# Mask attention phase: lift by a reduction, later store, the bias behind chunk 0's low halves, and a new order of small steps

## The reference

```python
xq = layer_norm(x, qn_w, qn_b)
ctx = layer_norm(context, cn_w, cn_b)
q = (xq @ q_w).reshape(B, N, H, D)            # H = 16 heads of D = 32
k, v = ...                                     # ctx @ kv_w
attn = jnp.einsum('bnhd,bmhd->bhnm', q, k) * scale
attn = softmax(jnp.where(xa_mask[:, None], neg, attn))
out = jnp.einsum('bhnm,bmhd->bnhd', attn, v).reshape(B, N, C)
x = x + (out @ proj_w + proj_b)
```

## Time and profile before

| what | value |
|---|---|
| median of three runs | 2689.25 us |
| the profiled execution | 2689.7 us, its span 2687.7 us, 2.0 us around it |
| mean granted TensorE clock | 0.992 |
| busy, share of the span | TensorE 97%, VectorE 74%, ScalarE 58%, GpSimd 34% |

### The profile page before, as it was taken

How to read it: one execution, slowest core, us unless ns; L and a number is a source line. 1 busy time by engine, 2 the same in 40 slices (tenths; PEclk the granted TensorE clock), 3 DMA queues, 4 the chain that set the end, 5 groups by cost and what they waited for, 6 DMA issues and landing times.

```text
span 2687.7 us, 67270 instructions
## 1 busy us (share of the span) xinstructions
PE 2602.1 (97%) x23144; PEld 2232.5 (83%) x23144; DVE 1983.5 (74%) x5443; ACT 1561.2 (58%) x4742; POOL 923.5 (34%) x1097
## 2 busy tenths in 40 slices
PE   5999999998999999999999999999999999999997
PEld 4777887886888888888888888888788888888886
DVE  6899999996544434443468888887788888888877
ACT  5777777776211111111267777777677676766764
POOL 4666666672100000000103333333433433434331
PEclk8999999999999999999999999999999999999999
DMA  5666676673402111111221111112321222212210
GB/s 163 164 159 162 172 175 160 170 203 88 130 32 63 47 47 37 56 47 47 79 87 48 47 47 52 49 47 79 98 81 62 79 79 76 87 62 89 75 47 24
DMA packets 313622, 236.12 MB, mean 88 GB/s; under 512 B 150736, under 2 KB 240848, under 8 KB 312656
## 3 DMA queue, kind: packets, MB, share of 16 engines
q1 hardware_dynamic: 313552, 235.22, 30.7%
HBM read 137.65 MB, written 63.96 MB: 75 GB/s over the span
## 4 chain that ended last, share of the span: by engine, by line
PE 76%; DVE 9%; ACT 8%; issue 5%; DMA 1%; POOL 1%; SPq 0%; DVEq 0%; ACTq 0%; POOLq 0%
PE cross_work L181 17%; PE mlp_acc L3308 13%; PE mlp_f L3290 13%; PE causal_work L181 10%; ACT mask_prob_even L964 3%; PE cross_scores L2301 3%; PE cross_scores L2278 2%; PE cross_attended L2331 2%; PE causal_scores L2301 2%; PE mask_work L181 2%; DVE mask_scores L1556 2%; PE causal_scores L2278 2%; PE causal_attended L2331 2%; ACT mask_prob L964 2%; PE cross_probsT L2301 1%
## 5 line engine op out<-in xcount | busy, mean ns | idle before, releaser
L3083 ACT ACTIVATE mlp_h<-mlp_f,mlp_b1col 128x512 f32<-128x512 f32 x128 | 88.3, 690 | 525.9 <-PE mlp_f L3290 525.9
L3290 PE MATMUL mlp_f<-mlp_xT_hi,mlp_w 128*128 128x512 f32 x1024 | 335.4, 389 | 0.9 <-DVE mlp_xT_lo L3176 0.9
L3190 DVE CAST mlp_hT_hi<-mlp_h 128x512 fp32r<-128x512 f32 x128 | 58.1, 454 | 369.9 <-ACT mlp_h L3083 369.8
L3308 PE MATMUL mlp_acc<-mlp_w,mlp_hT_hi 128*128 128x512 f32 x1024 | 315.2, 389 | 0.0
L964 ACT ACTIVATE cross_prob<-cross_scores,cross_low 128x256 f32<-128x256 f32 x512 | 237.1, 489 | 63.6 <-DVE cross_low L1550 63.6
L964 ACT ACTIVATE causal_prob<-causal_scores,causal_low 128x128 f32<-128x128 f32 (+1 forms) x512 | 210.3, 437 | 93.6 <-DVE causal_low L1556 93.6
L3290 PEld LDWEIGHTS mlp_f<-mlp_xT_hi,mlp_w 128*128 128x128 f32 x1024 | 192.3, 188 | 42.1 <-DVE mlp_xT_lo L3176 1.3
L3308 PEld LDWEIGHTS mlp_acc<-mlp_w,mlp_hT_hi 128*128 128x128 f32 x1024 | 192.2, 188 | 40.0
L181 PE MATMUL causal_work<-causal_xT_hi,causal_w 128*128 128x256 f32 x1008 | 217.0, 293 | 0.3 <-DVE causal_qk_parts L1506 0.3
L1556 DVE CUSTOM_DVE_ANT_0 mask_scores<-mask_scores,mask_mask 128x256 f32<-128x256 f32 x512 | 200.7, 452 | 21.8 <-PE mask_scores L2278 10.0
L731 POOL TENSOR_SCALAR causal_q<-all_own_head,causal_qk_parts 128x128 fp32r<-128x128 f32 x128 | 60.4, 483 | 406.0 <-DVE causal_qk_parts L1506 395.6
(11 more groups left out here) (368 smaller groups left out, 8108.9 us busy)
## 6 DMA issues: line engine op xcount, KB each, us to landing
cross_x_in<-after_attention SPq DMA_DIRECT2D x17, 512.0 KB, 4.1
mask_x_in<-in_x SPq DMA_DIRECT2D x16, 512.0 KB, 4.3
mask_c_in<-in_ctx SPq DMA_DIRECT2D x16, 512.0 KB, 4.8
mask_res<-in_x SPq DMA_DIRECT2D x16, 512.0 KB, 4.1
after_attention<-mask_res SPq DMA_DIRECT2D x16, 512.0 KB, 3.1
mlp_x<-after_attention SPq DMA_DIRECT2D x8, 1024.0 KB, 5.5
mlp_stage<-in_L_xattn_fc_w SPq DMA_DIRECT2D x8, 1024.0 KB, 5.6
after_layer<-mlp_y SPq DMA_DIRECT2D x8, 1024.0 KB, 4.3
```

The source lines that it names most:

```text
L3290: ins = pe.matmul(F1[m % 2][:], W[2 * (m // 4)][:, a, k, m % 4 * P:(m % 4 + 1) * P], xT[p][:, k, :], start=(k == 0 and n == 0), stop=(k == ...
L3308: ins = pe.matmul(ACC[t][:], hT[a][:, m % 2, t * P:(t + 1) * P], W[2 * (m // 4) + 1][:, p, m % 4, :], start=(m == 0 and n == 0), stop=(m = ...
```

## The change

Nothing that is computed changes. Its parts:

1. `low` gets a second column that GpSimd fills once with 10, and `lift` becomes a reduction over the pair (`tensor_reduce`, add) in place of `tensor_scalar`.
2. SyncE issues `cross_over(b, 2)` before `store(b - 1)`.
3. GpSimd does `add_bias(b)` behind `low_halves(b, 0)`, so in front of `values_left(b)`.
4. VectorE, loop: `normed(b, -1)`, `qk_lo(b, 1)`, `post_lo(b, 0)` instead of `post_lo(b, 0)`, `qk_lo(b, 1)`, `normed(b, -1)`; and `project(b, 0)` in front of `minima(b, 2)` instead of behind it.
5. ScalarE: `post_hi(b, 1)` in front of both `high_halves(b, 0, ...)`; in turn 0 the parts of v (`values`, `values_high`, `values_middle`) are made where the loop makes them, instead of later.
6. TensorE: `turn_sums(b, -1)` in front of `values(b, 1)` instead of in its middle; turn 0 makes `values(0, 1)` whole.
7. Opening: `front(1)` in front of `minima(0, 0)`, and `values(0, 0)` and `qk(0, 1)` earlier among the first exponentials. In turn 0 the first two `turn_over` stand in front of `minima(0, 2)`. In turn 15 the places where the MLP's opening may enter move.

```diff
-        low = r("low", [P, 4, TT])
+        low = r("low", [P, 4, TT, 2])
...
+            if crossing:
+                cross_over(b, 2)
             if not cross and prev:
                 store(b - 1)
-            if crossing:
-                cross_over(b, 2)
...
+            pool.memset(low[:], LIFT).then_inc(s["pool_chain"], 1)
...
                 low_halves(b, 0)
+                if prev:
+                    add_bias(b)
                 values_left(b)
...
+                post_hi(b, 1)
             high_halves(b, 0, 0)
-            if prev:
-                post_hi(b, 1)
             high_halves(b, 0, 1)
...
-            dve.tensor_scalar(lifted[:, h, :], low[:, h, :], LIFT, None, ALU.add).then_inc(s["lifted"], 1)
+            dve.tensor_reduce(lifted[:, h, :], low[:, h], AX_X, ALU.add).then_inc(s["lifted"], 1)
...
+            if prev:
+                minima(b, 0)
+                normed(b, -1)
+                qk_lo(b, 1)
+                post_lo(b, 0)
+                post_lo(b, 1)
...
+                project(b, 0)
...
             minima(b, 2)
-            if nxt and prev:
-                project(b, 0)
...
+            front(1)
             minima(0, 0)
-            front(1)
             qk_lo(0, 1)
...
+                turn_sums(b, -1)
             pe.wait_ge(s["v_ready"], 2 * b + 1)
-            values(b, 1, 0)
-            if prev:
-                turn_sums(b, -1)
-                values(b, 1, 1)
+            values(b, 1)
```

More of the change, by code:

```diff
@@ L390, in turned_before, with low_of @@
         return turned_by_pe(kind) * b + HC * (c // 2 if masked_ctx else c)
+    def low_of(u, qt):
+        return low[:, u % 4, qt, 0:1] if masked_ctx else low[:, u % 4, qt:qt + 1]
     def probs(b, c):
@@ L782, in turn @@
                     yield ROOM
-                if prev:
+                if not cur:
                     add_bias(b)
-                if not cur:
                     yield ROOM
@@ L791, in turn @@
                     gain(b + 1, 0)
-                if prev or not nxt:
-                    values_low(b)
+                values_low(b)
                 if nxt:
                     gain(b + 1, 1)
-                if not prev:
-                    values_low(b)
-                if nxt:
                     gain(b + 1, 2)
@@ L964, in exps @@
                 ins = act.activation(probs(b, c)[:, u % 4, qt, 0:w], SC[h][:, FROM[qt]:FROM[qt] + w], ACT.Exp,
-                                     bias=(lifted if crossed(c) else low)[:, u % 4, qt:qt + 1], scale=-1.0,
+                                     bias=lifted[:, u % 4, qt:qt + 1] if crossed(c) else low_of(u, qt), scale=-1.0,
                                      accum_out=sums[:, c // 2, qt, HC * (c % 2) + h:HC * (c % 2) + h + 1])
@@ L1074, in mask_turn @@
             exps(b, 7)
-            if prev:
-                values_middle(b)
+            values_middle(b)
             copy(b, 4)
@@ L1345, in scalar @@
             qk(0, 0)
-            for u in (0, 1, 2):
-                exps(0, u)
+            exps(0, 0)
+            exps(0, 1)
+            values(0, 0)
             qk(0, 1)
+            exps(0, 2)
             exps(0, 3)
-            values(0, 0)
             yield OPENED
@@ L1545, in masks_and_minima @@
                 dve.wait_ge(s["m_ready"], b + 1)
+                if isinstance(b, int) and b == 0:
+                    dve.wait_ge(s["pool_setup"], 1)
             if h == 0 and not cross:
@@ L1697, in mask_turn @@
         def mask_turn(b, prev, cur, nxt, after=True):
-            if cur and prev:
-                minima(b, 0)
-            if prev:
+            if not cur:
                 post_lo(b, 0)
-            if cur and prev:
-                qk_lo(b, 1)
-            if cur and not nxt:
-                yield ROOM
-            if prev:
                 normed(b, -1)
                 post_lo(b, 1)
-            if not cur:
                 yield ROOM
@@ L1724, in mask_turn @@
                 turn_over(b + 1, 3)
-            if not nxt:
+                project(b, 0)
+            elif nxt:
+                turn_over(b + 1, 0)
+                turn_over(b + 1, 1)
+            else:
                 yield ROOM
                 yield ROOM
-                if prev:
-                    project(b, 0)
+                yield ROOM
+                project(b, 0)
             minima(b, 2)
-            if nxt and prev:
-                project(b, 0)
-            else:
+            if not (nxt and prev):
                 over_sums(b, 0)
-            if not prev:
-                turn_over(b + 1, 0)
-                turn_over(b + 1, 1)
             if not nxt:
@@ L2510, in mask_turn @@
             attend(b, 0, 2)
-            if not nxt:
-                scores_taken(b, 11)
-                yield ROOM
             if prev:
@@ L2518, in mask_turn @@
                     project(b, 1, 1)
+            if not nxt:
+                scores_taken(b, 11)
+                yield ROOM
             if not (nxt and prev):
```

13 lines of the change are left out of this document (3 added, 10 removed).

## The result

The changed kernel takes 2706.18 us (median of 4 runs, 2703.33 to 2706.4) beside 2687.95 for the kernel before (median of 4): ratio 1.007, 95% interval 1.0051 to 1.0089. It is slower, by 18 us where 3 were forecast. Its profiled execution has a span of 2704.6 us against 2687.7, and a mean granted clock of 0.988 against 0.992. A second set of 5 runs on another chip gave 2704.45 beside 2685.91, ratio 1.0069 (1.0056 to 1.0083), span 2701.3.

The account below looks back on a forecast made before the run. It took the chain of waits through TensorE, VectorE's lift and ScalarE, 38.35 us a turn, as the bound. Loop +14, opening -6, end -8 and clock +3 made +3: 2692 us, range 2680 to 2707.

Parts of the forecast that it names:

- The stall: ScalarE's values_middle waits for GpSimd's values_left behind the bias, so scores(b, 2) starts 2.4 us later each turn (2.2 to 2.7).
- The lift: VectorE's first lift of chunk 2 shortens from 1.44 to 0.17 us as a reduction: -1.3 us a turn.
- The wide copy: Copy of over_sums in the turn's second half, 1.22 us against 0.43 undisturbed: taken as -0.2 us a turn.
- The loop: Each mask-phase turn: 2.4 - 1.3 - 0.2 = +0.9 us, bounds +0.2 to +1.8; 14 us over 14 turns.
- the lower one: Lower bound per turn, +0.2 us: wait of 2.2, copy undisturbed, 0.1 more by chunk 1's earlier start.
- The clock: TensorE's new 2.4 us pause before scores(b, 2) lowers the clock in a quarter of the turns: +3 us in all.
- The first rival: The clock falls in every turn behind TensorE's new pause: +14 in place of +3, 2703 us; chance 0.22.
- a clock that drops turn by turn: Named sign of a wrong prediction: TensorE's clock not staying at 1.00 around the pause before scores(b, 2).
- The opening: Turn 0: front(1) first gets the DMA transposes issued earlier, shortening TensorE's 11.88 us pause: -6 us (-2 to -7).
- the end: Last transposes issued ahead of the store, removing TensorE's 4.93 us wait, plus clock and turn 15: -8 us (-4 to -9).
- Project, normed, post_lo and turn_sums: VectorE's and TensorE's reordered loop steps: hidden or off the chain, so no gain or loss counted.
- The second half of the turn: GpSimd reaches turned_hi some 3 us later, but nobody waits for its late work except the copy of over_sums.

Follow-up runs that it names:

- experiment 1: The changed kernel with GpSimd adding the bias ahead of chunk 0's low halves again: 2665.27 us, ratio 0.9925.
- experiment 3: The kernel before with only the lift changed to tensor_reduce (second column of low and its memset): 2682.02 us, ratio 0.9987.
- experiment 2: The changed kernel with the lift by tensor_scalar again, everything else kept: 2717.26 us, ratio 1.0116.
- experiments 9: The changed kernel with the opening's old order, minima(0, 0) ahead of front(1): 2710.34 us, ratio 1.0091.
- experiment 8: The kernel before with only the store moved behind the last transposes: 2688.36 us, ratio 0.9964.
- experiment 7: The changed kernel with values_middle moved behind copy(b, 6) on ScalarE, bias still behind the low halves: 2692.02 us, ratio 0.9975.
- experiment 6: The changed kernel with the bias ahead of the low halves and TensorE repeating four transposes five more times: 2697.22 us, ratio 0.9995.
- experiment 4: The kernel before with only the bias moved behind chunk 0's low halves: 2732.46 us, ratio 1.0175.

## Why the prediction came out as it did

Its range held, by 0.8 us at the upper end, and its time was 14 us too low. The places that it named were right; the size of the loop was not. Step by step:

- *The stall, +2.4 us a turn.* Right in place, waiting instruction and size: ScalarE idle 2.27, TensorE 2.36, and without it the turn falls to 36.98 (experiment 1). With the clock, the place of the bias is worth 39.78 - 36.95 = 2.83 a turn.
- *The lift, -1.3 us a turn.* This is the term that was mis-sized. The reduction is as short as taken (0.149 to 0.160 in all 128), and beside GpSimd's normalising, where the old form took 0.70, it takes 0.15; so the trace agrees with the Trainium skill ("SBUF — State Buffer", section "Who interferes with whom"), by which a `tensor_reduce` never contends for the port pair that VectorE shares with GpSimd. Against a long turn the term holds: 38.35 + 2.36 - 1.29 (1.44 to 0.15) = 39.42, and a turn at full clock takes 39.43. But its worth was read from one turn of the long kind, and the turns are not alike: four of twelve had the short first lift already. Measured against the mean: 37.81 to 37.20, **-0.6 a turn** without the stall (experiment 3), and 40.63 to 39.78, -0.85 beside it (experiment 2). TensorE's own work caps the saving as well, but by less: the earlier trace rows, 48.0 of 50 us, leaves 1.5 us of pause in a turn of 38.35, room for all of the 1.3.
- *The wide copy, -0.2.* It did not come. In the turns at full clock the first wide copy takes 1.3 us, beside 1.23 in the long turns before; in the turns in which the clock fell it takes 0.43 to 0.83. Turns 5 and 6 of the changed kernel:

```profile
263.36 1.29 DVE L1562 COPY mask_rs<-mask_rs 128x512 f32<-128x512 f32 x1
...
303.46 0.43 DVE L1562 COPY mask_rs<-mask_rs 128x512 f32<-128x512 f32 x1
```

- *The loop, +0.9 a turn.* In the changed kernel a turn at full clock is 39.43, beside the 39.2 forecast; the 0.2 is what the wide copy was to bring. The larger error is in what it is compared with: 37.81 in the mean, not 38.35. That is +1.6 a turn, some 23 us where 14 stood. The bounds were off too: the terms named for the lower one, 2.2 - 1.3 - 0.8 - 0.1, make 0.0 and not +0.2.
- *The clock, +3.* Chance and price were both off: it falls behind the stall in 9 turns rather than 3 or 4, but costs 0.57 us in each (40.0 against 39.43), not 1. Together 5. The first rival's mechanism (it falls after most pauses) held, and one of the prediction's own signs of being wrong, a clock that drops turn by turn, came in two turns of three. That the rival's time of 2703 comes near is luck: it counts 14 for the clock where 5 came, and the loop's +23 makes up for it.
- *The opening, -6, and the end, -8.* Right: -5.9 and -7.8; experiments 9 and 8 give the steps named for them.
- *Project, normed, post_lo and turn_sums, nothing.* Nearly right: with the store they are worth 0.25 a turn without the stall (experiments 1 and 3); beside the stall they were not tried alone.
- *The second half of the turn, nothing.* Right as long as the first stall covers it; experiment 7 shows that a delay of 2 us was waiting underneath.

The sum by measured terms: loop 23 + clock 5 - 6 - 8 = +14, where the spans differ by 16.9. Of the remaining 3 us half lie between `scores(1, 0)` and `scores(2, 2)`, where turn 1 of the kernel before had a first lift of 0.20 us and so little to gain, and half behind the phase (+1.4), without a cause traced.

## What to carry to other kernels

Before a turn's saving is priced, list the period of many turns and not of one, and set the saving against what the busiest engine has idle in a turn: work added to a full engine is paid in full (experiment 6), and a saving elsewhere gives no more than that idle time. When work of a helper engine is moved behind another piece, look for every engine that waits for what comes after it; taking the first of these waits away may only uncover the next. Small jobs with no early reader, such as a bias, belong in the helper's idle time, if their data is there.

## What the runs showed that was not expected

- A pause of 2.36 us ahead of the same work left the granted clock at 1.00 in some turns and was followed by 0.50 in others, 8 of 12, and one of 1.96 us in turn 1 was followed by 0.50. Before, one of 2.3 was harmless and one of 3.1 was not the earlier trace rows. The length of a pause alone did not decide it.
- A small `tensor_scalar` for the same two numbers a row took 0.29 and 1.42 us in the kernel before, 1.45 in experiment 8 and 1.70 in experiment 4. Every one of these lifts that takes over 0.18 us, 243 in the five versions with the old form, ends 0.02 to 0.03 us behind the end of a GpSimd operation that runs beside it: the 0.29 behind the first one, the 1.42 behind the third in a row. So it waits for one, two or three of them. What decides how many is not shown: in turns 2 and 12 of the kernel before it starts 0.28 us into the same operation, the three operations end at the same distances from its start within 0.01 us, and it takes 1.42 us once and 0.29 the other time.
- Moving a store on SyncE (experiment 8) changed the mix of short and long turns from 4 and 8 to none and 12. A kernel with such an operation in its chain can gain or lose 7 us by an edit that has nothing to do with it.
- The kernel before had medians of 2685.4, 2685.9 and 2698.4 on three chips. That the mix of turns differs there is a guess; no profile of it was taken beside these runs.
